# The mid stage of a two-layer scan network: C spread as three bf16 parts, convolution taps folded into a projection, output product on ScalarE and GpSimd

## The reference

```python
xz = einsum('bhwc,ec->bhwe', xp, in_proj_w); x_in, x_gate = split(xz, 2)
xc = conv2d(x_in, conv2d_w, depthwise 3x3)
x_act = silu(xc)                          # 4 images, 4096 positions, 96 channels
xz = einsum('bld,ed->ble', x_act, in_w)
xm, z = split(xz, 2)
xm = silu(conv1d(xm, c1_w, 3 taps, causal, depthwise) + c1_b)
dbl = einsum('bld,ed->ble', xm, xp_w)     # 6 values for dt, 16 for B, 16 for C
dt = softplus(einsum('blr,dr->bld', dt_r, dt_w) + dt_b)
# over the positions t, for each channel d and each of 16 states n:
h = exp(dt[t, d] * A[d, n]) * h + dt[t, d] * xm[t, d] * B[t, n]
y[t, d] = sum over n of h * C[t, n]
y = (y + xm * D) * silu(z)
```

## Time and profile before

| | |
|---|---|
| median of 3 runs | 1581.51 us (1580.91 to 1585.74) |
| profiled execution, time | 1586.61 us |
| its span | 1584.7 us |
| TensorE busy, instructions | 1235.0 us, 3822 |
| VectorE busy, instructions | 1220.5 us, 1226 |
| ScalarE busy, instructions | 1110.7 us, 1643 |
| GpSimd busy, instructions | 905.2 us, 451 |
| mean granted TensorE clock | 0.789 |

### The profile page before, as it was taken

The page is one execution under the profiler, slowest core; times in us unless marked ns, Lnnn a source line. Parts: engine busy times, 40 slices in busy tenths (PEclk is TensorE's granted clock), DMA queues, the critical chain, the costliest instruction groups (busy, mean ns, idle before and its releaser), DMA issues. The chain is left out here.

```text
span 1584.7 us, 14386 instructions
## 1 busy us (share of the span) xinstructions
PE 1235.0 (78%) x3822; PEld 436.1 (28%) x3822; DVE 1220.5 (77%) x1226; ACT 1110.7 (70%) x1643; POOL 905.2 (57%) x451
## 2 busy tenths in 40 slices
PE   3899935656554777777898998989989898776995
PEld 2344301111102555422222222222222221112663
DVE  1655638989882777505999999999999999993775
ACT  2677366767642777668888888988889888631664
POOL 2400049999993333227788777887778877750000
PEclk8999955555556999876988789887898978555997
DMA  5444390201002333229777877778777887615572
GB/s 147 118 141 121 98 184 24 106 0 48 6 40 73 95 99 88 75 75 213 183 167 173 191 178 170 171 173 190 174 177 168 177 186 164 147 37 129 121 177 58
DMA packets 136428, 200.53 MB, mean 127 GB/s; under 512 B 26739, under 2 KB 68770, under 8 KB 135564
## 3 DMA queue, kind: packets, MB, share of 16 engines
q1 hardware_dynamic: 133740, 196.15, 51.1%
q10 hardware_dynamic: 2160, 2.61, 0.6%
q0 software_dynamic: 448, 0.85, 0.2%
HBM read 145.93 MB, written 53.63 MB: 126 GB/s over the span
## 5 line engine op out<-in xcount | busy, mean ns | idle before, releaser
L1349 POOL TENSOR_TENSOR m_ub<-m_dlb,m_bt 128x1536 f32<-128x1536 f32 x128 | 440.4, 3442 | 145.7 <-DVE m_h L1703 139.7
L1703 DVE TENSOR_TENSOR_SCAN m_h<-m_qa,m_state,m_ub 128x512 f32<-128x512 f32 x384 | 463.7, 1261 | 53.3 <-POOL m_ub L1349 51.7
L1665 ACT ACTIVATE m_qa<-m_dlb,k_a 128x512 f32<-128x512 f32 x384 | 255.2, 685 | 109.5 <-DVE m_h L1703 104.0
L1714 DVE TENSOR_TENSOR m_g<-m_h,m_qc 128x1536 f32<-128x1536 f32 x128 | 221.7, 1732 | 18.4 <-issue 12.5
L1532 PE MATMUL m_qc<-m_bcr,k_selc 32*128 32x512 f32 x256 | 167.8, 739 | 83.0 <-DVE m_g L1714 82.7
L1074 POOL TENSOR_TENSOR b_u<-b_dl,b_z 128x1024 f32<-128x1024 f32 x48 | 124.4, 2594 | 155.9 <-DMA b_z<-scratch_z 151.5
L1549 PE MATMUL m_qy<-m_g,k_seld 128*32 128x512 f32 x768 | 168.4, 739 | 0.0
L939 PE MATMUL b_qb<-b_bc,k_pack_sel 96*128 96x512 bf16 x96 | 58.9, 613 | 100.7 <-DVE b_u L1021 92.4
L1085 POOL TENSOR_TENSOR b_y<-b_y,b_g 128x1024 f32<-128x1024 f32 x48 | 129.7, 2703 | 3.9 <-DVE b_g L1043 3.9
L1473 PE MATMUL m_qf<-m_cva,k_conv 113*96 113x504 f32 (+1 forms) x192 | 126.0, 808 | 5.0 <-PEq L1105 5.0
L1532 PEld LDWEIGHTS m_qc<-m_bcr,k_selc 32*128 32x128 f32 x256 | 42.9, 209 | 208.4 <-issue 190.0
(11 more groups left out here) (178 smaller groups left out, 2286.5 us busy)
## 6 DMA issues: line engine op xcount, KB each, us to landing
m_dlb<-scratch_dldu SPq DMA_DIRECT2D x128, 384.0 KB, 9.7
m_bt<-scratch_brow SPq DMA_DIRECT2D x128, 256.0 KB, 5.9
scratch_dldu<-m_dldu SPq DMA_DIRECT2D x32, 384.0 KB, 4.9
scratch_z<-a_z SPq DMA_DIRECT2D x24, 256.0 KB, 6.0
...
```

Source lines behind the costliest of these rows:

```text
L1349: nc.gpsimd.tensor_tensor(ub[k % 3][:], dlb[u % 2][:, J:2 * J, :], bcast(bt[u % 2][:, n, :], J), ALU.mult).then_inc(ub_ready, 1)
L1665: nc.scalar.activation(q_a[:, j, :], dlb[u % 2][:, j, :], ACT.Exp, scale=G["a1"][:, j, n:n + 1]).then_inc(da, 1)
L1703: nc.vector.tensor_tensor_scan(h[k % 3][:, j, :], q_a[:, j, :], ub[k % 3][:, j, :], state[:, k % NS, j:j + 1], ALU.mult, ALU.add).then_inc ...
L1714: nc.vector.tensor_tensor(g[k % 2][:], h[k % 3][:], bcast(q_c[:], J), ALU.mult).then_inc(read, 1)
```

## The change

It has three parts, all in the second layer's mixer, and the setup for them.

1. **C.** Instead of one float32 matmul over 32 rows, the spread is one bf16 matmul over 112 rows. C is held as three bf16 tables that add up to it, in rows 32, 64 and 96 of a new tile `m_cp`. ScalarE writes the rounded C (L1696), GpSimd subtracts it (L1385), ScalarE rounds the rest (L1704), GpSimd subtracts again (L1395). `selc` becomes bf16 with three blocks.
2. **Taps.** The three causal taps are folded into the projection of u: three weight matrices `u_taps`, and three float32 matmuls that add up in `m_qm`, each reading `m_xa` shifted by one position. `m_xa` gets five buffers with two columns of history, and ScalarE's copy writes the sum directly to `m_acc`. ScalarE's three taps and GpSimd's two sums go.
3. **Output product.** VectorE's `outputs` goes. ScalarE copies `m_qy` to `m_yq` (L1737), ahead of the window of silus, and GpSimd multiplies with `m_sz` (L1406). The store of y moves from the second to the fourth step on SyncE's queue. A helper `alone` on GpSimd waits until its own earlier work has ended.

```diff
+            def alone(drives, products, results):
...
+            def rest_of(v):
...
+                pool.wait_ge(top_out, v + 1)
...
+                nc.gpsimd.tensor_tensor(rest[mid], bcr[v % 4][top], cp[v % 4][top], ALU.subtract).then_inc(rest_out, 1)
...
+            def least_of(v):
...
+                pool.wait_ge(middle_out, v + 1)
...
+                nc.gpsimd.tensor_tensor(cp[v % 4][lo], rest[mid], cp[v % 4][mid], ALU.subtract).then_inc(parted, 1)
...
+            def outputs(v):
...
+                pool.wait_ge(y_out, v + 1)
+                pool.wait_ge(sz_ready, v + 1)
...
+                nc.gpsimd.tensor_tensor(yo[v % 2][:], yq[:], sz[v % 5][:], ALU.mult).then_inc(y_ready, 1)
...
-                if s == 1:
-                    conv_sum(t + 3)
+                if s == 2:
+                    outputs(t - 1)
+                if s == 0:
+                    alone(k + 3, t + 2, t - 1)
+                    rest_of(t + 2)
+                if s == 3:
+                    alone(k + 3, t + 3, t)
+                    least_of(t + 2)
...
-                nc.tensor.matmul(q_m[:], G["l1_min_x"][:], xa[v % 2][:], start=True, stop=True).then_inc(u_mm, 1)
+                for k in range(3):
+                    last = nc.tensor.matmul(q_m[:], G["u_taps"][:, k, :], xa[v % HIST][:, k:k + CH], start=(k == 0),
+                                            stop=(k == 2))
+                last.then_inc(u_mm, 1)
...
-                pe.wait_ge(bc_out, u + 1)
+                pe.wait_ge(parted, u + 1)
...
-                nc.tensor.matmul(q_c[:], G["selc"][DI:P, 4 * n:4 * n + 4, :], bcr[u % 4][DI:P, :], start=True, stop=True).then_inc(c_mm, 1)
+                nc.tensor.matmul(q_c[:], G["selc"][:, 4 * n:4 * n + 4, :], cp[u % 4][:], start=True, stop=True).then_inc(c_mm, 1)
...
                 if n == 0 and u >= 1:
-                    pe.wait_ge(y_ready, u)
+                    pe.wait_ge(y_out, u)
...
-                    act.wait_ge(summed, 2 * b + 2)
+                    act.wait_ge(u_out, b + 1)
...
+                nc.scalar.activation(acc[:], q_m[:], ACT.Identity).then_inc(u_out, 1)
...
-            def taps(v):
...
+                nc.scalar.activation(cp[v % 4][DI:DI + NS, :], q_g[DI:DI + NS, :], ACT.Identity).then_inc(top_out, 1)
...
+                nc.scalar.activation(cp[v % 4][64:64 + NS, :], rest[64:64 + NS, :], ACT.Identity).then_inc(middle_out, 1)
...
+                nc.scalar.activation(yq[:], q_y[:], ACT.Identity).then_inc(y_out, 1)
...
                 if s == 1:
+                    y_evict(t - 1)
                     window(t + 4, t + 3)
                 if s == 2:
+                    tail_of(t + 5)
                     u_of(t + 4)
+                    middle(t + 2)
...
-            def outputs(v):
-                if not exists(v):
-                    return
-                dve.wait_ge(added, 4 * v + 4)
```

More of the change, by code:

```diff
@@ L65 @@
 DL = 4
+C_PARTS = (32, 64, 96)
 def lead(eng, *sems):
@@ L1283, in mid1_phase @@
         cva, cvb, cv_first = G["cva"], G["cvb"], G["cv_first"]
-        xa, gt, yo = ([m.sb(f"m_{n}{r}", [DI, CH]) for r in range(2)] for n in ("xa", "gt", "yo"))
-        u1 = [m.sb(f"m_u{r}", [DI, 2 + CH]) for r in range(HIST)]
-        tp = [m.sb(f"m_tp{k}", [DI, CH]) for k in range(3)]
+        gt, yo = ([m.sb(f"m_{n}{r}", [DI, CH]) for r in range(2)] for n in ("gt", "yo"))
+        yq = m.sb("m_yq", [DI, CH])
+        xa = [m.sb(f"m_xa{r}", [DI, 2 + CH]) for r in range(HIST)]
         acc = m.sb("m_acc", [DI, CH])
@@ L1290, in mid1_phase @@
         bcr = [m.sb(f"m_bcr{r}", [P, CH]) for r in range(4)]
+        cp = [m.sb(f"m_cp{r}", [DI + NS, CH], BF16) for r in range(4)]
+        rest = m.sb("m_rest", [64 + NS, CH])
         dldu = [m.sb(f"m_dldu{r}", [DI, 2, CH]) for r in range(2)]
@@ L1329, in _ @@
             for r in range(HIST):
-                nc.gpsimd.memset(u1[r][:, 0:2], 0.0).then_inc(zeroed, 1)
+                nc.gpsimd.memset(xa[r][:, 0:2], 0.0).then_inc(zeroed, 1)
             nc.gpsimd.memset(state[:], 0.0).then_inc(zeroed, 1)
+            for r in range(4):
+                nc.gpsimd.memset(cp[r][:], 0.0).then_inc(zeroed, 1)
             pool.wait_ge(zeroed, NZ - 4)
@@ L1449, in step @@
                     load_drive(t + 2)
+                    store_y(t - 1)
             turns(step)
@@ L1502, in z_of @@
                 pe.wait_ge(u_out, v + 1)
-                nc.tensor.matmul(q_m[:], G["l1_min_z"][:], xa[v % 2][:], start=True, stop=True).then_inc(z_mm, 1)
+                nc.tensor.matmul(q_m[:], G["l1_min_z"][:], xa[v % HIST][:, 2:2 + CH], start=True, stop=True).then_inc(z_mm, 1)
             def u_of(v):
@@ L1684, in step @@
                     rows_out(t + 2)
-                    taps(t + 3)
             turns(step)
```

132 lines of the change are left out of this document (79 added, 53 removed).

## The result

| | time, median (runs) | ratio to before, 95% interval | profiled span | first to last scan |
|---|---|---|---|---|
| before | 1581.37 us (6) | 1 | 1584.7 us | 702.1 us |
| after | 1574.18 us (6) | 0.9946 [0.993, 0.9963] | 1573.1 us | 683.0 us |

The change makes the kernel faster by 0.54%, 7.2 us between the medians. The forecast was 1584 us and no measurable change. The profiled spans differ by 11.6 us, because the profiled run of before lies 5 us above its median.

The account below looks back on a forecast made before the run. VectorE (DVE) was taken to bound the kernel, at no less than 21.34 us a unit. Terms -40 + 34 + 3 + 0 + 3 + 1.3 + 1 = +2.3 us gave 1584 us; range 1564 to 1602, the forecast's own 1577 to 1590.

Parts of the forecast that it names:

- the price of u at half clock: TensorE, third step: u's three float32 pairs at half clock make DVE wait 1.8 us in 19 of 28 units, +34 us.
- The waits for the spread of C: DVE before the C product: the bf16 spread ends earlier and removes 15 of 18.4 us of waits.
- The output product: Leaves DVE: 32 x 0.58 = 18.6 us of work and the 6.8 us wait before it go.
- ACT's window: The m_qy copy lengthens ACT's longest stretch, delaying the first decay 0.1 us a unit: +3 us, between 0 and 6.
- POOL: GpSimd's added subtractions and output product fit, since its drives run two steps ahead: 0 us.
- Filling: Four units before the first scan: two more u pairs delay ACT, +3 us, between 0 and 11.
- Setup: More diagonals, a cleared table, three matmuls and a DVE product: +1 us, between 0 and +4.
- Tail: At the end the last y passes ACT's copy and POOL instead of DVE: +1.3 us.
- B: Rival: every unit's u meets the low clock, 28 x 1.8 = 50 us, giving 1603 us; chance 0.18.
- A: Rival: low clock stays where it is, a third of units having it on u, 18 us, giving 1568 us; chance 0.29.
- C: Rival: POOL's order binds, its first subtraction waiting for ACT's m_cp; 19 us more, 1606 us; chance 0.06.
- D: Rival: TensorE's clock doesn't fall at all, leaving -40 and the small terms, 1550 us; chance 0.05.

Follow-up runs that it names:

- the kernel with the early copy: Changed kernel with ScalarE's copy of m_qy moved from ahead of the silu window (second step) to the end of the first step: 1550.9 us, ratio 0.9793.

## Why the prediction was wrong, step by step

The kernel got 7.2 us faster where no change was forecast, and its 1574.2 us lie below the forecast's own range, 1577 to 1590.

**The failed step is the price of u at half clock**: +34 us, from 19 units of 28 at 1.8 us; measured were 9.3 us. The share was too low, the price far too high. Every unit has u matmuls at half clock. But the price was the sum 3 x 1.82 + 1.84 + 0.61 = 7.9 us, which lets the low level last for the whole chain. In the trace it ends before the chain does, in short stretches of PE around the worst unit (length, busy, clock, DMA share, GB/s):

```profile
1020.80:1023.30 2.50, 1.36 (x7) 1.00 0.42 121
1023.30:1030.10 6.80, 6.50 (x8) 0.50 0.78 210
1030.10:1033.50 3.40, 3.40 (x13) 1.00 1.05 225
```

The full-clock chain is 3.87 us (measured in the kernel with the early copy; the estimate was 4.1). Of the 7.1 us in the worst unit 6.5 are at half clock, and half of them, 3.2, is what the clock adds: 3.87 + 3.2 = 7.1. In the two other units the low level began earlier, over a stretch in which TensorE waited anyway, and cost the chain only 2.3 and 1.9. The Trainium skill, page "TensorE: Matmul & The Clock Gate", section "HAM oscillation — how this bites in real kernels", prices a throttled time at half of its length; by that rule the 6.5 us cost 3.2, and the trace agrees. What the prediction lacked is when a low stretch begins and ends, against the chain. The earlier trace rows showed one as long as 3.3 us and the step went on to 7.9 us of chain at that level. The margin, 6.1 us, was right (measured 7.09 - 0.96 = 6.13).

**The waits for the spread of C**: -15 of 18.4. In the stage 16.1 went and 9.3 came, all of the latter behind u; the term itself was right, as taps and C together show (2.3 us left).

**The output product**: -18.6 for its work and -6.8 for its wait. The stage had 31 of them before its last scan, 18.0 us, and DVE's busy time fell by 16.1. The missing 1.9 us are, as an estimate, the overlap of 0.08 us (1023.51 + 0.66 against 1024.09) that an instruction behind a wait loses: there are 26 more waits of DVE (45 against 19), which makes 2.1. The wait before the product was 4.1 in the stage, and 2.7 in its last unit.

**ACT's window**: +3, bounds 0 and 6. It cost 9.5 us, outside the bounds, 0.35 us in every unit instead of 0.1. The forecast end of the first decay was 0.02 us after DVE's need; the copy takes 0.61 us before the table load, where nothing overlaps it, instead of 0.5, and what the other 0.2 us consist of was not separated. A margin of 0.02 us should have been priced by the rounding of the numbers behind it, over 27 units. And the true cost was larger than the wait: the copy also keeps u back by 0.6 us. Moving it gave 19.8 us between the first and the last scan.

**POOL**: 0, right. **Filling** +3: 2.0 measured. **Setup** +1: 1.0, which shows little, since this start lies anywhere from 674.5 to 683.4 us in the profiles. **Tail** +1.3: 2.1 to the next stage's first product, where the copy and POOL's product take this:

```profile
1423.44 0.59 ACT L1737 ACTIVATE m_yq<-m_qy 96x512 f32<-96x512 f32 x1 [7.27 <-PE m_qy L1609]
1424.11 1.26 POOL L1406 TENSOR_TENSOR m_yo<-m_yq,m_sz 96x512 f32<-96x512 f32 x1 [15.88 <-ACT m_yq L1737]
```

**The rivals.** B had the mechanism (all units meet the low level, three units repeat in step with the clock) and the wrong price. A had the nearer number, 1568, with a wrong premise: the low level did not stay where it was, u's mean rose from 779 to 1015 ns. C and D did not come. With u's term at its measured 9.3 us and ACT's at 9.5, the prediction's own sum would be 2.3 - 24.7 + 6.5 = -15.9 us, against -11.6 in the profiled runs.

**The signs.** A unit took 683.0 / 31.9 = 21.4 us, under the 21.5 that was to speak for A or D, and neither held: this sign couldn't tell a cheap low level from a rare one. The sign for ACT's stretch, over 0.2 us a unit for m_qa, came true.
